# A deformable convolution's gathers on GpSimd: the limit on items under way counts landed gathers, two items back, in place of PE's turns, and the buffers' wait is written out in every item

## The chip, the cores and the metric

One core of a Trainium2 chip. Times are microseconds of device time for one execution. The kernel before takes 948.3 us, the median of three runs (947.69 to 948.37).

## What is computed

Input x is float32, 4 images of 128 channels by 48 x 48. Cut to what matters:

```python
def deform(x):                       # x normalised by groups of 4 channels
    om = conv3x3(x, w_offset) + b_offset          # 27 channels: dy, dx, mask of 9 taps
    py, px = grid_y + dy, grid_x + dx             # a place for each pixel and tap
    cols = bilinear(x, py, px) * sigmoid(mask)    # four corners, weighted
    out = einsum('bckhw,ock->bohw', cols, w_conv) + b_conv
    return relu(batchnorm(out))                   # statistics over all images

x = x + deform(groupnorm(x))
x = x + conv3x3(groupnorm(x), w) + b
```

## The kernel before, in words

The pixels of the four images are cut into 24 chunks of 384 (three tiles of 128 pixels). The host lays out a table with one row for each place of the padded image; a row holds the 128 channels of all four corners of that place, 2 KB. For one tap and one tile of 128 pixels a single indirect DMA, issued by GpSimd (L388), gathers 128 such rows into the buffer `g[:, k, t]`, 256 KB. There are 9 x 3 such buffers, so one chunk fills all of them, and the whole kernel makes 648 gathers.

An **item** is three gathers whose sums are made together. In chunks 1 to 22 an item is one tap of all three tiles, nine items to a chunk. In chunk 0 and in chunk 23 (`BY_TILE`) an item is three taps of one tile, and the last chunk has ten items, as its last three taps are split 2 and 1. All items are counted through from 0 to 216; `first_item(c)` is the number of a chunk's first.

For each item, in this order:

- GpSimd issues the three gathers; their landing adds to the semaphore `gathered[i]`, one for each place i in the chunk. `landed(c, i)` is the value that it has when item i of chunk c is there.
- The vector engine (`sum_item`) multiplies three corners by their weights in place (L952), ScalarE the fourth (`scale_item`, L682), both after waiting for `gathered[i]`. Then the vector engine adds the four (L965, L968, L971) into `acc`, one of five. Each item adds 4 to `sum_step`.
- PE turns the sums by transposing (`turn_item`, L507) and adds 1 to `turned`; ScalarE copies them into `cols` (L663); PE multiplies them by the weights (`conv_item`, L495) one or two items later.

Beside the items, between their steps, the vector engine works out the places and weights of the next chunk (L847 to L883 for chunks 0 and 1, `later_indices` after that), and PE the offsets' convolution (L443). Those orders are written out by hand and are the same before and after.

GpSimd's queue is strictly in order. At a chunk's first item it waits for the chunk's indices (`idx_ready` for chunks 0 and 1, after that a value of `sum_step` in item 3 of the chunk before). At an item it waits, if need be, for `sum_step`, so that the sums that read the buffers it takes are done: in chunk 1 these are the sums of items 6 to 8, for the first item those of item 6; between later chunks it is the item nine back, and in chunk 23 it is three to seven back. Lastly it waits for `turned`: item s starts when item s-4 is turned (`LEAD = 4`). As a turn comes after its item's sums, the wait for `sum_step` is left out where the wait for `turned` covers it, which is nearly everywhere.

SP loads x: image 0 first, then the weights, then images 1, 2 and 3 (1152 KB each, L341; each of them waits for the one before it) and the second convolution's weights (L342), while the first gathers are under way.

When all items are done, the batch statistics, the ReLU, the second group normalisation and the second convolution follow (from about 830 us), in a form with four products for two columns; GpSimd then mixes columns (L327) and adds (L319).

Of the kernel before, what the change touches and what calls it, by code (L numbers as in the profile page):

```python
# [34 lines left out]

TILE_ROWS = 3

LEAD = 4

SUMS, TURNS = 5, 3  # L40

# [44 lines left out]
def items(c):  # L86

    if c not in BY_TILE:
        return [[(k, t) for t in range(TILES)] for k in range(TAPS)]
    return [[(k, t) for k in taps] for t in range(TILES) for taps in (LAST_SETS if (c, t) == (ALL - 1, TILES - 1) else TAP_SETS)]  # L90


def first_item(c):
    return sum(len(items(i)) for i in range(c))


def all_items():
    return [(c, i) for c in range(ALL) for i in range(len(items(c)))]
# [6 lines left out]
def last_use(c, unit):  # L105

    return next(i for i, units in enumerate(items(c)) if unit in units)
# [6 lines left out]
def sums_at(c, i, slot=3):  # L114

    return 4 * item(c, i) + slot + 1
# [22 lines left out]
def landed(c, i):  # L139

    return 16 * sum(len(items(e)[i]) for e in range(c + 1) if i < len(items(e)))
# [21 lines left out]
def build(nc, x_d, tab_d, woff_d, wconv_d, w1_d, boff_d, par_d, grid_d, out_d):  # L163

    with ExitStack() as ctx:
# [6 lines left out]
        def sem(name):  # L172
            return ctx.enter_context(nc.semaphore(name))
# [95 lines left out]
        gathered = [sem(f"gathered{i}") for i in range(max(len(items(c)) for c in range(ALL)))]  # L269
        scaled = sem("scaled")  # L270
        sum_step = sem("sum_step")
        turned = sem("turned")
# [44 lines left out]
        def add_band(eng, b, j):  # L317
            s = b * HW + j * BP
            return eng.tensor_tensor(x[:, s:s + BP], x[:, s:s + BP], o[:, s:s + BP], ALU.add)  # L319

        def mix(eng, b, h, m):
            first, rows = (0, BR + 2) if h == 0 else (h * BR + 2, BR)
            src = xn[:, b % IMAGES * PW + first:b % IMAGES * PW + first + rows, :]
            d0, d2 = src[:, :, 0:W:2], src[:, :, 2:PW:2]
            d1, d3 = src[:, :, 1:W:2], src[:, :, 3:PW:2]
            p, q, op = ((d0, d2, ALU.subtract), (d1, d2, ALU.add), (d2, d1, ALU.subtract), (d1, d3, ALU.subtract))[m]
            return eng.tensor_tensor(mixed[:, m, first:first + rows, :], p, q, op)  # L327

        @block.sync
        def _(sp):  # L330
            for i in range(0, CHUNKS, 2):
                sp.dma_start(x[:, X0[i] * CP:X0[i + 1] * CP], x_d[:, 0, X0[i] * CP:X0[i + 1] * CP]).then_inc(x0_in[i], 16)
            sp.dma_start(woff[:], woff_d).then_inc(wo_in, 16)
            sp.dma_start(boff[:], boff_d).then_inc(wo_in, 16)
            sp.dma_start(grid[:], grid_d).then_inc(gr_in, 16)
            sp.dma_start(wconv[:], wconv_d).then_inc(wc_in, 16)
            sp.dma_start(params[:], par_d).then_inc(wc_in, 16)
            for b in range(1, B):
                if b > 1:
                    sp.wait_ge(xr_in[b - 2], 16)  # L340
                sp.dma_start(x[:, b * HW:(b + 1) * HW], x_d[:, b]).then_inc(xr_in[b - 1], 16)  # L341
            sp.dma_start(w1[:], w1_d).then_inc(w1_in, 16)  # L342
            for n in range(B * BANDS):
                sp.wait_ge(finished, 2 * n + 2)
                sp.dma_start(out_d[:, n * BP:(n + 1) * BP], x[:, n * BP:(n + 1) * BP]).then_inc(stored, 16)
            sp.wait_ge(stored, 16 * B * BANDS)

        @block.gpsimd
        def _(pl):
            xn4 = xn[:].rearrange("p (b r) w -> p b r w", b=IMAGES)  # L350
            pl.memset(wz[:], 0.0).then_inc(consts, 1)
            pl.memset(eps[:], EPS).then_inc(consts, 1)
            pl.memset(last_stats[:, 0:1], float(B * HW - 2 * P)).then_inc(consts, 1)
            pl.memset(gshift[:], 0.0).then_inc(consts, 1)
            pl.memset(gavg[:], 1.0 / GROUP).then_inc(consts, 1)
            pl.memset(ident[:], 0.0).then_inc(consts, 1)
            gv = gavg[:].rearrange("p (a b) -> p a b", b=GROUP)
            pl.wait_ge(consts, 5)
            pl.affine_select(out=gv, in_=gv, compare_op=ALU.is_ge, fill=0.0, base=0,
                             pattern=[[-GROUP, P // GROUP], [0, GROUP]], channel_multiplier=1).then_inc(consts, 1)  # L360
            pl.wait_ge(consts, 7)
            pl.affine_select(out=gv, in_=gv, compare_op=ALU.is_ge, fill=0.0, base=GROUP - 1,  # L362
                             pattern=[[GROUP, P // GROUP], [0, GROUP]], channel_multiplier=-1).then_inc(consts, 1)
            pl.affine_select(out=ident[:], in_=ident[:], compare_op=ALU.not_equal, fill=1.0, base=0,
                             pattern=[[-1, P]], channel_multiplier=1).then_inc(consts, 1)
            pl.memset(xn4[:, :, 0:PW:PW - 1, :], 0.0).then_inc(consts, 1)
            pl.memset(xn4[:, :, 1:1 + H, 0:PW:PW - 1], 0.0).then_inc(consts, 1)

            for c in range(ALL):
                if c < 2:  # L370
                    pl.wait_ge(idx_ready, 2 * c + 1)
                else:
                    pl.wait_ge(sum_step, sums_at(c - 1, *IDX_SLOT))
                for i, units in enumerate(items(c)):
                    if c == 0 and i == len(TAP_SETS):
                        pl.wait_ge(idx_ready, 2)
                    if c:

                        used = max(last_use(c - 1, unit) for unit in units)
                        if i < len(items(c - 1)):  # L380
                            used = max(used, i)
                        if first_item(c - 1) + used > first_item(c) + i - LEAD:
                            pl.wait_ge(sum_step, (first_item(c - 1) + used + 1) * 4)
                    if first_item(c) + i >= LEAD:

                        pl.wait_ge(turned, first_item(c) + i - LEAD + 1)
                    for k, t in units:
                        pl.indirect_dma_start(  # L388
                            out=g[:, k, t].rearrange("p q c -> p (q c)"), out_offset=None, in_=tab_d,
                            in_offset=bass.IndirectOffsetOnAxis(ap=idx[:, c % 2, t, k:k + 1], axis=0),  # L390
                        ).then_inc(gathered[i], 16)

            def add(b):
                for j in range(0, BANDS, 2):
                    pl.wait_ge(relued, b * BANDS + (BAND_ORDER.index(j) + 1))
                    add_band(pl, b, j).then_inc(added, 1)

            def mix_band(b, h):
                pl.wait_ge(normed, b * BANDS + (h + 1))
                if b:  # L400

                    pl.wait_ge(conv1, MIX * ((b - 1) * BANDS + min(h + 2, BANDS)))
                for m in range(MIX):
                    mix(pl, b, h, m).then_inc(mixed_ready, 1)

            add(0)
            for b in range(B - 1):
                mix_band(b, 1)
                mix_band(b, 2)
                add(b + 1)  # L410
                mix_band(b, 3)
                mix_band(b + 1, 0)
            for h in range(1, BANDS):
                mix_band(B - 1, h)
# [711 lines left out]
```

## Time and profile before

| what | before |
|---|---|
| median of 3 runs | 948.3 us |
| the profiled execution | 948.03 us |
| its span, first to last instruction | 946.3 us |
| busy, PE / vector engine / ScalarE / GpSimd | 748.1 / 795.8 / 375.0 / 669.2 us |
| GpSimd's gathers (L388), 648 | 613.3 us busy, 212.9 us idle ahead of them |
| moved by the gathers' queue | 169.91 MB |
| first and last gather start | 16.09 and 828.58 us |

The span is cut by what the trace records; the execution's own time is 1.7 us longer. A row of the profile for a group of instructions gives the line, engine and operation, what is written and read, the count, busy time, the mean of one in ns, and the idle time of that engine just before, with what ended most of it. A timeline row gives start, duration, engine, line, operation, operands, count, and in brackets the idle time before and its releaser; "issue" is idle time in which the engine waited for nothing that the profile shows. "DMA to landing" is the time from a gather's start on GpSimd until its data is there and its semaphore raised.

### The profile page before, as it was taken

To read this page: it belongs to the slowest core of one execution; us is meant where nothing else is said; L and a number is where in the kernel's file an instruction comes from. 1 tells how busy PE (TensorE), PEld (TensorE's weight loads), DVE (VectorE), ACT (ScalarE), POOL (GpSimd) and SP (SyncE) were. 2 spreads that over 40 slices of the span, in tenths; PEclk is the share of its full clock that TensorE was granted. 3 is DMA by queue.
4 is the path that set the end of the run, shared out by engine and by line. 5 is a ranking of instruction groups with operands and counts; after the bars stand their busy time and mean duration, and the time that the engine had idled before them with its cause. 6 is when DMAs were issued, how large, how long until landed. Compare 5 with 4: busy or idle time off the path is not lost.

```text
span 946.3 us, 8953 instructions
## 1 busy us (share of the span) xinstructions
PE 748.1 (79%) x2436; PEld 351.1 (37%) x2436; DVE 795.8 (84%) x1533; ACT 375.0 (40%) x1026; POOL 669.2 (71%) x731
## 2 busy tenths in 40 slices
PE   7688778877877877787778788778678776879998
PEld 5342322322322322232223323223222222667776
DVE  3789989888889989888899899888889889866664
ACT  3433435434333435433434345343343344453210
POOL 3777777777777777777777777777777777737551
PEclk9876778878768778976887878787797785599999
DMA  7777777777777777777777777777777777711111
GB/s 274 233 200 209 211 210 210 210 209 212 209 211 211 209 212 209 212 209 210 210 210 210 210 212 210 210 212 209 211 209 211 209 210 211 210 33 51 51 51 50
DMA packets 56246, 181.39 MB, mean 192 GB/s; under 512 B 11012, under 2 KB 12036, under 8 KB 55812
## 3 DMA queue, kind: packets, MB, share of 16 engines
q0 software_dynamic: 51840, 169.91, 62.5%
q1 hardware_dynamic: 3924, 10.32, 2.9%
q10 hardware_dynamic: 432, 0.59, 0.2%
q8 instruction: 19, 0.31, 0.1%
q14 instruction: 31, 0.25, 0.1%
HBM read 176.06 MB, written 4.72 MB: 191 GB/s over the span
## 4 chain that ended last, share of the span: by engine, by line
POOL 36%; PE 18%; DVE 18%; issue 14%; DMA 12%; ACT 1%; DVEq 0%; POOLq 0%; ACTq 0%
POOL g L388 36%; DMA g<-corner_table,idx 12%; DVE g L952 7%; PE TP L593 2%; PE PA L593 2%; PE CO L593 2%; PE CO L495 2%; PE TP L507 2%; DVE PA L965 2%; DVE PA L968 2%; DVE acc L971 2%; PE OMT L443 2%; PE VU L593 1%; PE OMT L593 1%; PE PA L438 1%
## 5 line engine op out<-in xcount | busy, mean ns | idle before, releaser
L388 POOL DMA_INDIRECT g<-corner_table,idx x648 | 613.3, 947 | 212.9 <-issue 180.7
L682 ACT ACTIVATE PA<-g,wt 128x128 f32<-128x128 f32 x642 | 203.4, 358 | 459.1 <-DMA g<-corner_table,idx 256.1
L952 DVE TENSOR_TENSOR g<-g,PA 128x1152 f32<-128x1152 f32 (+1 forms) x217 | 291.4, 1343 | 51.5 <-DMA g<-corner_table,idx 50.9
L495 PE MATMUL CO<-cols,wcs 128*128 128x384 f32 (+1 forms) x504 | 260.2, 619 | 78.7 <-ACT cols L663 77.5
L507 PE MATMUL TP<-ident,acc 128*128 128x128 f32 x648 | 146.9, 347 | 101.3 <-DVE acc L971 98.7
L443 PE MATMUL OMT<-xn,woff 128*27 128x384 f32 (+2 forms) x450 | 187.3, 534 | 3.2 <-DVE wt L878 2.0
L495 PEld LDWEIGHTS CO<-cols,wcs 128*128 128x128 f32 x504 | 92.8, 238 | 223.5 <-ACT cols L663 193.7
L507 PEld LDWEIGHTS TP<-ident,acc 128*128 128x128 f32 x648 | 89.1, 171 | 224.9 <-DVE acc L971 211.3
L965 DVE TENSOR_TENSOR PA<-g,PA 128x384 f32<-128x384 f32 x214 | 120.6, 564 | 19.1 <-ACT PA L682 1.2
L968 DVE TENSOR_TENSOR PA<-g,PA 128x384 f32<-128x384 f32 x214 | 119.8, 560 | 5.9
L971 DVE TENSOR_TENSOR acc<-g,PA 128x384 f32<-128x384 f32 x214 | 118.0, 552 | 5.9
L663 ACT ACTIVATE cols<-TP 128x384 f32<-128x384 f32 (+1 forms) x217 | 101.3, 467 | 8.8 <-PE TP L507 8.6
L443 PEld LDWEIGHTS OMT<-xn,woff 128*27 128x27 f32 x450 | 38.9, 110 | 67.5 <-issue 62.4
L327 POOL TENSOR_TENSOR g<-xn 128x288 f32<-128x288 f32 (+1 forms) x60 | 41.4, 724 | 31.7 <-ACT xn L769 30.6
L481 PE MATMUL CO<-vt,ut 9*128 9x384 f32 (+1 forms) x56 | 38.5, 784 | 0.0
L646 ACT ACTIVATE std<-OMT,eps 128x1 f32<-128x1 f32 x4 | 1.0, 262 | 50.4 <-PE OMT L424 50.4
L438 PE MATMUL PA<-gavg 128*128 128x128 f32 x128 | 18.1, 305 | 2.9 <-POOL gavg L362 2.6
L319 POOL TENSOR_TENSOR x<-x,o 128x576 f32<-128x576 f32 x8 | 12.1, 1524 | 10.8 <-ACT o L757 10.7
L438 PEld LDWEIGHTS PA<-gavg 128*128 128x128 f32 x128 | 17.2, 217 | 3.1 <-POOL gavg L362 2.6
L464 PE MATMUL VU<-ident,vsum 128*9 128x128 f32 x72 | 12.2, 279 | 6.5 <-DVE g L952 5.7
L481 PEld LDWEIGHTS CO<-vt,ut 9*128 9x128 f32 x56 | 12.9, 284 | 9.4 <-issue 9.4
L451 PEld LDWEIGHTS OMT<-ident,om 27*128 27x128 f32 x72 | 8.3, 179 | 20.2 <-issue 19.2
(148 smaller groups left out, 525.9 us busy)
## 6 DMA issues: line engine op xcount, KB each, us to landing
g<-corner_table,idx POOLq DMA_INDIRECT x648, 3.7
out_dram<-x SPq DMA_DIRECT2D x16, 288.0 KB, 2.1
x<-x_dram SPq DMA_DIRECT2D x3, 1152.0 KB, 7.8
x<-x_dram ACTq DMA_DIRECT2D x3, 192.0 KB, 4.2
x<-x_dram SPq DMA_DIRECT2D x3, 192.0 KB, 3.9
wconv<-wconv_dram SPq DMA_DIRECT2D x1, 576.0 KB, 5.0
w<-w_dram SPq DMA_DIRECT2D x1, 576.0 KB, 10.0
grid<-grid_dram SPq DMA_DIRECT2D x1, 162.0 KB, 4.2
```

What stands on the lines that cost most here:

```text
L388: pl.indirect_dma_start(out=g[:, k, t].rearrange("p q c -> p (q c)"), out_offset=None, in_=tab_d, in_offset=bass.IndirectOffsetOnAxis(ap=i ...
L443: last = nc.tensor.matmul(OM[:, first * W:(first + rows) * W], woff[:, k, :], xn[:, row + k // 3:row + k // 3 + rows, k % 3:k % 3 + W], st ...
L481: nc.tensor.matmul(co_bank(c, t)[:, lo:hi], ut[:, c // CHUNKS % 2, :], vt[:, lo:hi], start=True, stop=False)
L495: last = nc.tensor.matmul(co_bank(c, t)[:, t * P:t * P + size], wcs[:, c // CHUNKS % 2, k, :], cols[:, s % TURNS, n * P:n * P + size], sta ...
L507: last = nc.tensor.transpose(TP[s % 2][:, n * P:(n + 1) * P], acc[:, s % SUMS, n, :], ident[:])
L593: last = nc.tensor.matmul(MX[h % 2][m][:, 0:HB], w, mixed[:, m, r:r + BR, :], start=(ky == 0), stop=(ky == 2))
L663: nc.scalar.activation(cols[:, s % TURNS, 0:size], TP[s % 2][:, 0:size], ACT.Copy).then_inc(copied, 1)
L682: last = nc.scalar.activation(first[:, n] if s < LAST_SUMS else g[:, k, t, 0, :], g[:, k, t, 0, :], ACT.Copy, scale=wt0[:, c % 2, t, k:k + 1])
L952: nc.vector.tensor_tensor(corners[:, :, 1:4, :], corners[:, :, 1:4, :], weights[:, :, 1:4].unsqueeze(3).to_broadcast([P, size, 3, P]), ALU ...
L965: nc.vector.tensor_tensor(some, corners[:, :, 1, :], some, ALU.add).then_inc(sum_step, 1)
L968: nc.vector.tensor_tensor(some, corners[:, :, 2, :], some, ALU.add).then_inc(sum_step, 1)
L971: nc.vector.tensor_tensor(acc[:, s % SUMS, 0:size, :], corners[:, :, 3, :], some, ALU.add).then_inc(sum_step, 1)
```

## The change

The wait for `turned` goes. In its place an item waits until the item two back has landed (`AHEAD = 2`), whichever chunk that is in. The wait for `sum_step` stands in every item from chunk 1 on, without the test that left it out. Gathers, their order, their number and all other engines' programs stay as they are.

```diff
-LEAD = 4
+AHEAD = 2
...
+            order = all_items()
             for c in range(ALL):
                 if c < 2:
                     pl.wait_ge(idx_ready, 2 * c + 1)
...
                     if c:
 
                         used = max(last_use(c - 1, unit) for unit in units)
                         if i < len(items(c - 1)):
                             used = max(used, i)
-                        if first_item(c - 1) + used > first_item(c) + i - LEAD:
-                            pl.wait_ge(sum_step, (first_item(c - 1) + used + 1) * 4)
-                    if first_item(c) + i >= LEAD:
-
-                        pl.wait_ge(turned, first_item(c) + i - LEAD + 1)
+                        pl.wait_ge(sum_step, (first_item(c - 1) + used + 1) * 4)
+                    s = first_item(c) + i
+                    if s >= AHEAD:
+
+                        pl.wait_ge(gathered[order[s - AHEAD][1]], landed(*order[s - AHEAD]))
                     for k, t in units:
                         pl.indirect_dma_start(
...
```

## Rows read from the trace of the kernel before

**Rows 1.** Page, the costliest groups

```profile
L388 POOL DMA_INDIRECT g<-corner_table,idx x648 | 613.3, 947 | 212.9 <-issue 180.7
```

**Rows 2.** Busy time by stage: PE, PEld, DVE, ACT, POOL, clock, DMA share, GB/s

```profile
100.00:200.00 100.00, 76.80 (x235) 29.97 (x235) 89.09 (x172) 44.56 (x124) 75.63 (x81) 0.81 0.74 210
```

**Rows 3.** Timeline of GpSimd, line 388

```profile
18.75 0.95 POOL L388 DMA_INDIRECT g<-corner_table,idx  x1 [0.30 <-issue]
...
23.75 0.95 POOL L388 DMA_INDIRECT g<-corner_table,idx  x1 [0.30 <-issue]
...
36.74 0.95 POOL L388 DMA_INDIRECT g<-corner_table,idx  x1 [2.04 <-PE TP L507]
...
52.98 0.94 POOL L388 DMA_INDIRECT g<-corner_table,idx  x1 [1.54 <-issue]
...
119.25 0.95 POOL L388 DMA_INDIRECT g<-corner_table,idx  x1 [0.30 <-issue]
...
120.50 0.94 POOL L388 DMA_INDIRECT g<-corner_table,idx  x1 [0.30 <-DVE g L952]
...
828.58 0.95 POOL L388 DMA_INDIRECT g<-corner_table,idx  x1 [0.30 <-issue]
```

**Rows 4.** Timeline of the other engines, 26 to 52 us

```profile
26.61 1.36 DVE L952 TENSOR_TENSOR g<-g,PA 128x1152 f32<-128x1152 f32 x1 [3.81 <-DMA g<-corner_table,idx]
...
35.98 0.49 PE L507 MATMUL TP<-ident,acc 128*128 128x128 f32 x3
...
39.53 1.35 DVE L952 TENSOR_TENSOR g<-g,PA 128x1152 f32<-128x1152 f32 x1
...
41.56 0.56 DVE L965 TENSOR_TENSOR PA<-g,PA 128x384 f32<-128x384 f32 x1 [0.68 <-ACT PA L682]
...
51.66 0.55 DVE L971 TENSOR_TENSOR acc<-g,PA 128x384 f32<-128x384 f32 x1
```

**Rows 5.** Line 388 by source: landing of all; of the gather at 18.75; at 22.50

```profile
DMA to landing us min/median/max: 3.3/3.7/7.8
...
DMA to landing us min/median/max: 7.8/7.8/7.8
...
DMA to landing us min/median/max: 6.7/6.7/6.7
```

**Rows 6.** Timeline around a late landing

```profile
614.50 0.96 POOL L388 DMA_INDIRECT g<-corner_table,idx  x1 [0.30 <-issue]
...
619.52 0.95 POOL L388 DMA_INDIRECT g<-corner_table,idx  x1 [0.30 <-PE TP L507]
...
620.26 1.35 DVE L952 TENSOR_TENSOR g<-g,PA 128x1152 f32<-128x1152 f32 x1 [1.95 <-DMA g<-corner_table,idx]
```

**Rows 7.** Line 388 by source: nine stretches of 34 us, from 84 us on

```profile
DMA to landing us min/median/max: 3.5/3.7/4.8
...
DMA to landing us min/median/max: 3.4/3.7/4.7
...
DMA to landing us min/median/max: 3.4/3.7/5.4
...
DMA to landing us min/median/max: 3.4/3.7/4.4
...
DMA to landing us min/median/max: 3.5/3.7/4.6
...
DMA to landing us min/median/max: 3.5/3.7/4.4
...
DMA to landing us min/median/max: 3.5/3.7/5.0
...
DMA to landing us min/median/max: 3.5/3.6/5.7
...
DMA to landing us min/median/max: 3.4/3.7/4.9
```

**Rows 8.** DMA queues, 614 to 622 us: packets, MB, share

```profile
q8 instruction: 1, 0.02, 0.7%
```

## The prediction

> **What bounds the kernel now.** I read the page first: GpSimd's line 388, 648 indirect gathers at 947 ns with 0.30 us of idle ahead of each, is the costliest group, and only its "issue" idle is large [rows 1]. Then the table by stage: from 100 to 200 us GpSimd runs 81 gathers at 75.6%, while the vector engine is busy 89%, PE 77% and the DMA engines 74% [rows 2]. Eighty-one gathers in 100 us is one per 1.25 us (0.95 busy and 0.30 of issue), and the timeline shows that pitch, as from 119.25 to 120.50 [rows 3]. So the stage of the gathers, 16 to 830 us, is bound by GpSimd making descriptors. Everything else is paced by it. From the gather at 52.98 to the last at 828.58 there are 620 pitches, 775.0 us at 1.25; the trace has 775.6. The stage thus holds 0.6 us of stalls after 53 us, and two larger ones ahead of that: 2.04 - 0.30 = 1.74 us at 36.74 (item 5, put down to PE's turn) and 1.54 - 0.30 = 1.24 us at 52.98 (item 9, the first of chunk 1) [rows 3]. That is all an easier limit could win. Anything that stalls GpSimd afterwards is lost for good, as it has no slack.
>
> **What the change removes.** Item s no longer waits for the turn of item s-4. In chunk 0 that frees 1.74 us at item 5. But item 9 takes buffers that item 6 has to be done with, a wait that stands before and after. Item 6's last addition starts at 51.66 and takes 0.55, so it ends at 52.21, and the gather starts at 52.98 [rows 3, 4]. The vector engine goes from 39.53 to there nearly without a pause (four items' sums and chunk 1's indices). So item 9 could not have started sooner than 52.98, however early items 5 to 8 were: the 1.74 us are worth nothing. Of the 0.6 us left I take 0.2 as winnable.
>
> **What it adds at the start.** Item 2 now waits until item 0 has landed. Item 0's third gather starts at 18.75 and lands 7.8 us later, at 26.55, while the ordinary gather takes 3.7 [rows 3, 5]; the vector engine's wait for it ends at 26.61 [rows 4]. The large loads of x lie beside it, in both kernels. Item 2 started at 23.75 before [rows 3]. A released gather starts some 0.27 us after its releaser: item 5 did, after a turn that began at 35.98 and took 0.49 [rows 3, 4]. Item 2 then starts at 26.55 + 0.28 = 26.83, a new stall of 3.08 us. Item 1's last gather, issued at 22.50, lands at 29.2 [rows 5], ahead of item 3's place at 30.58: no second stall. From 26.83, item 9's first gather (21 pitches of 1.25 on) is due at 53.08, not 52.98. The vector engine moves too: item 4's third gather starts at 36.83 and lands at 40.53, so its first product starts at 40.55 in place of 39.53 [rows 4]. Before, its second step was held to 41.56 by ScalarE; now it comes at 40.55 + 1.35 + 0.11 = 42.01, so the later chain moves by 0.45 and item 6's sums end at 52.66. If the gather follows that by the same 0.77 us as before (52.98 - 52.21), item 9 starts at 53.43. **Term: +0.45 us** (bounds +0.1, at the pitch alone, to +0.5).
>
> **What the written-out buffer wait costs.** From chunk 1 on nearly every item then has two waits in place of one. Where both are satisfied early I cost this at nothing: the first item of a chunk has two waits already, and its gather at 120.50 comes 1.25 us behind the one at 119.25, like any other [rows 3]. What covers it is GpSimd working on the gather before. If the cover were gone, 200 items would pay each time. What the buffer wait asks for, sums nine items back, is long done except at item 9.
>
> **What the new limit costs in steady state.** Item s-2's third gather starts four pitches, 5.00 us, ahead of item s. If released late, item s starts a lag after the landing. The nearest rows for the lag are two: 0.27 us at item 5, which has one wait, and 0.77 us at item 9, which has several and was released by one that is not the gather's own [rows 3, 4]. I take 0.77, as from chunk 1 on each item has two waits and the new one is written second, as the wait that released item 9 was. The Trainium skill's page "Perfetto Trace Analysis", section "Identifying Dependency Chains", says that instructions with several waits may get separate EventSemaphore instructions ahead of them; by that the second wait is one more step for the queue after its release, and the 0.77 agrees.
>
> With 0.77 a gather may take 4.23 us to land before it stalls the item two behind. The ordinary 3.7 is hidden. But nine stretches of 34 us after chunk 0 have a maximum above that: 4.8, 4.7, 5.4, 4.4, 4.6, 4.4, 5.0, 5.7 and 4.9 us [rows 7]. Read one by one, each is the third gather of its item, the one with the least room. The worst starts at 614.50; the vector engine waits for it until 620.26, while item 160 had started at 619.52, so the new wait would have held that one [rows 6]. These are no accidents of one run, I think: in this stretch one 16 KB packet of the instruction queue q8 passes the DMA engines [rows 8], and the same goes for eight of the nine; I take it for an engine's program being loaded, and only GpSimd's program changes, so they should return at about the same items. Sum: 43.9 - 9 x 4.23 = **+5.8 us**. With the lag of 0.28 the limit is 4.72 and five remain, 0.08 + 0.68 + 0.28 + 0.98 + 0.18 = +2.2 us. With a lag of 1.0, near ordinary landings of 4.0 to 4.2 count too: replaying all 648 starts and landings gives +8.5.
>
> The sum: 0.45 + 5.8 - 0.2 = +6.0 us. The profiled execution took 948.03 us (span 946.3), 0.27 below the median of 948.3. The stage after 830 us starts on the last item and only moves along. 948.03 + 6.0 = **954.0 us**, 0.6% more.
>
> **Rivals.** (a) *Short lag.* The queue sees the landing as fast as item 5 saw its turn: 0.45 falls to 0.1, 5.8 to 2.2, so 948.03 + 2.1 = 950.1. For it speaks item 5, against it item 9. It decides at items 42, 86, 115 and 131, which would show no stall. (b) *Ordinary landings are caught too.* If the lag is 1.0 or more, or the delays fall on more items, the sum is +8.5 and the time 956.5. For it: the room is only 5.00 - 3.7 - 0.77 = 0.5 us; against it, nothing in the trace shows a lag over 0.77. (c) *No change.* Landings are in time everywhere, and GpSimd keeps its 1.25: the start costs 0.1, 0.2 is won, 948.0 to 948.5. The mechanism's place is the room of 5.00 us: it decides if no third gather takes over 4.2. Against it stand the nine maxima, unless these were chance. The Trainium skill's "DMA: Bandwidth & Descriptors", section "Anatomy of one DMA", gives a transfer on this path as 2.0 us plus bytes over 436e3; by that, an estimate from its figures, a gather of 262144 bytes lands in 2.6 us and the wait is never late. The rows have 3.7 with outliers to 5.7, which decide against it. (d) *Faster.* There would have to be more than 0.6 us to win after 53 us, or a vector engine that reaches item 6's sums sooner; at most 947.4. No row speaks for it.
>
> **How the numbers follow.** Chances: the forecast (lag 0.5 to 0.9) 0.55; (a) 0.19; (b) 0.12; (c) 0.11; (d) 0.03. A difference of 0.2%, 1.9 us, is about what a measurement of this kernel tells from none, so the line to slower is 950.2. The forecast and (b) are wholly slower, and half of (a) is: 0.55 + 0.12 + 0.10 = 0.77; within 0.2%: the other half of (a), (c) and most of (d), 0.21; faster 0.02. The range goes from (a) at its low side, 949.9, to (b) with 1 us of noise in how many late landings one run has, 957.5; (c) and (d) are left out.
>
> **What would show it.** In the changed profile: item 2's first gather at about 26.8 with some 3.1 us of idle, and none at item 5; item 9 at 53.1 to 53.4; GpSimd's waits naming its own gathers instead of PE's turns; eight to ten stalls of 0.2 to 1.5 us at the first gather of items two behind a late landing (25, 42, 70, 86, 115, 131, 140, 160, 176); the last gather at 834 to 835 in place of 828.58. The pitch elsewhere stays 1.25 and the stretch from the last gather to the end keeps its length. A pitch above 1.25 at every third gather would prove me wrong on the cost of a second wait, and stalls at many items with 3.7 us landings would prove me wrong on the lag.

## The result, and the profile after

The changed kernel takes 955.94 us, the median of five runs (952.68 to 956.26), where before takes 948.37 (947.69 to 949.8): a ratio of 1.0074, with a 95% interval of 1.0057 to 1.0091. It is slower, by 0.7%, some 7 us. The profiled execution is the quickest of the five, 952.68 us with a span of 950.7; that is 4.65 us above the profiled one of before, and 3.3 below its own median.

The page has the same busy times as before. What changed is how GpSimd's idle time ahead of its gathers ends [rows 1], and the chain that ended last: GpSimd had 36% of it and the gathers' transfers 12%; now they have 14% and 46%. The first fence is from the page of the changed kernel, the chain by engine and the group of the gathers; the second is the list of its waits on GpSimd (us in total, times, longest us).

```profile
DMA 46%; DVE 18%; POOL 14%; PE 12%; issue 9%; ACT 1%; POOLq 0%; DVEq 0%; ACTq 0%
...
L389 POOL DMA_INDIRECT g<-corner_table,idx x648 | 613.4, 947 | 217.8 <-issue 136.9
```

```profile
POOL g L389 <- issue: 136.9, 446, 0.6
POOL g L389 <- DMA g<-corner_table,idx: 49.3, 146, 3.0
```

Idle time rose by only 4.9 us, from 212.9 to 217.8. Of the 49.3 us put down to transfers, most is 0.30 us at a time, the ordinary pitch with the landing named as releaser. So the shares of the chain mislead here; what counts is where a pitch is longer than 1.25 us. The timeline of the changed kernel on GpSimd shows it, with the first products of two items and the sum that item 9 waited for (these answer to [rows 3, 4, 6]):

```profile
26.60 1.35 DVE L953 TENSOR_TENSOR g<-g,PA 128x1152 f32<-128x1152 f32 x1 [3.43 <-DMA g<-corner_table,idx]
26.77 0.94 POOL L389 DMA_INDIRECT g<-corner_table,idx  x1 [2.95 <-DMA g<-corner_table,idx]
...
53.44 0.55 DVE L972 TENSOR_TENSOR acc<-g,PA 128x384 f32<-128x384 f32 x1
...
54.75 0.94 POOL L389 DMA_INDIRECT g<-corner_table,idx  x1 [2.03 <-DVE acc L972]
...
617.62 0.96 POOL L389 DMA_INDIRECT g<-corner_table,idx  x1 [0.30 <-DMA g<-corner_table,idx]
...
623.13 1.35 DVE L953 TENSOR_TENSOR g<-g,PA 128x1152 f32<-128x1152 f32 x1 [1.70 <-DMA g<-corner_table,idx]
623.87 0.94 POOL L389 DMA_INDIRECT g<-corner_table,idx  x1 [1.55 <-DMA g<-corner_table,idx]
...
833.64 0.95 POOL L389 DMA_INDIRECT g<-corner_table,idx  x1 [0.88 <-DMA g<-corner_table,idx]
```

Item 2 starts at 26.77, just after item 0's landing. Item 9 starts at 54.75 in place of 52.98. The gather at 617.62 is the third of item 158, the one that was late before too; it lands at 623.11, when the vector engine starts on it, and item 160 starts 0.76 us later, at 623.87, with 1.25 us of stall. The last gather starts at 833.64, 5.06 us later than the 828.58 of before. By the starts of all 648 gathers:

| stretch | later than before, us |
|---|---|
| first gather (16.47, was 16.09) | 0.38 |
| from there to item 9's first | 1.39 |
| first gathers of later items, sum of their pitches less 1.25 each (3.33, was 0.45) | 2.88 |
| second and third gathers, the same (0.56, was 0.15) | 0.41 |
| sum | 5.06 |

Five of the later items hold 2.1 us: 86, 115, 146, 160 and 176, each two behind a late third gather. Item 216, the last, holds 0.58 us more; why is told further below.

### The profile page after: what moved, and what is told of

It reads as the page before. It is cut to its first block, busy times and chain, and to the rows that moved or that the text cites. A ratio compares the mean times of both kernels' runs of the same rounds, so it can differ in the third digit from the quotient of the medians.

```text
span 950.7 us, 9138 instructions
## 1 busy us (share of the span) xinstructions
PE 748.7 (79%) x2436; PEld 351.3 (37%) x2436; DVE 796.4 (84%) x1533; ACT 375.1 (39%) x1026; POOL 669.3 (70%) x731
## 4 chain that ended last, share of the span: by engine, by line
DMA 46%; DVE 18%; POOL 14%; PE 12%; issue 9%; ACT 1%; POOLq 0%; DVEq 0%; ACTq 0%
DMA g<-corner_table,idx 46%; POOL g L389 14%; DVE g L953 7%; PE TP L594 2%; PE PA L594 2%; PE CO L594 2%; DVE PA L966 2%; DVE PA L969 2%; DVE acc L972 2%; PE VU L594 1%; PE OMT L594 1%; DVE bst L835 1%; PE PA L439 1%; PE CO L496 0%; ACT PA L683 0%
## 5 line engine op out<-in xcount | busy, mean ns | idle before, releaser
L389 POOL DMA_INDIRECT g<-corner_table,idx x648 | 613.4, 947 | 217.8 <-issue 136.9
```

The source lines that it names most:

```text
L389: pl.indirect_dma_start(out=g[:, k, t].rearrange("p q c -> p (q c)"), out_offset=None, in_=tab_d, in_offset=bass.IndirectOffsetOnAxis(ap=i ...
```

## The experiments

Ratios are to the kernel before on the same chip. Kernels 1 to 4 shared a chip and its runs of before, as did 5 to 8, and 9 to 12.

**1 and 2. The order of the two waits, and the written-out wait alone.** In the compiled program an item's first wait sits in the gather instruction itself, and the others in a separate semaphore instruction ahead of it. In the changed kernel from chunk 1 on the gather holds the buffers' wait and the separate instruction the landing.

```diff
                 for i, units in enumerate(items(c)):
+                    s = first_item(c) + i
+                    if s >= AHEAD:
+                        pl.wait_ge(gathered[order[s - AHEAD][1]], landed(*order[s - AHEAD]))
...
                         pl.wait_ge(sum_step, (first_item(c - 1) + used + 1) * 4)
-                    s = first_item(c) + i
-                    if s >= AHEAD:
-                        pl.wait_ge(gathered[order[s - AHEAD][1]], landed(*order[s - AHEAD]))
```

The chunk's wait for indices moves behind the landed one as well, so that this is first at every item.

> The changed kernel with its two kinds of waits in the other order: in each item the wait for the landing is written first and so becomes the gather's own wait, and the buffers' wait becomes the separate instruction ahead of it. Theory (a late landing costs its lateness plus the lag of the queue, and the lag is 0.75 us behind a separate wait but 0.27 behind the gather's own): lag 0.25 to 0.3 at late items, only landings over 4.7 us cost, and the time is 2 to 4 us below the changed kernel, 951 to 953.5. Rival A (a landed wait costs the same wherever it stands): within 1 us of the changed kernel, 955 to 957, lag still 0.75. Rival B (the start in chunk 0 makes the loss): the same as the changed kernel, since chunk 0 has one wait in both.

Measured: 950.73 us, ratio 1.0027 (1.0015 to 1.004); the loss falls from 7 to under 3 us. The program has the same instructions, and only the order of two waits differs. Its timeline around the same late gather, the third of item 158:

```profile
616.04 0.95 POOL L389 DMA_INDIRECT g<-corner_table,idx  x1 [0.31 <-issue]
...
621.54 1.35 DVE L953 TENSOR_TENSOR g<-g,PA 128x1152 f32<-128x1152 f32 x1 [1.86 <-DMA g<-corner_table,idx]
621.78 0.94 POOL L389 DMA_INDIRECT g<-corner_table,idx  x1 [1.03 <-DMA g<-corner_table,idx]
```

The landing is as late (5.5 us), but item 160 follows it by 0.26 us and not by 0.76. Its four stalls behind a late landing (items 25, 70, 115 and 160) all have that lag, and the changed kernel's all have 0.76. (The trace has landings to 0.01 us; the view gives them to 0.1.) Rivals A and B fall.

The second kernel goes back to PE's turns, with `pl.wait_ge(turned, s - LEAD + 1)` at `LEAD = 4` for the landed wait and the rest of the change kept.

> One part alone: the limit by PE's turns, four items back, as before, with the buffers' wait written out in every item. So nearly every item has a separate wait for turns and an own wait for sums. Theory: written-out waits cost nothing when they are satisfied early, but at each chunk's item 6 the turn comes only just in time before, and behind a separate wait a lag of 0.75 in place of 0.27 makes stalls there: up to 22 times 0 to 0.5 us, 949 to 956, pitch elsewhere 1.25. Rival C (the added instructions themselves cost queue time): every third pitch is longer than 1.25 by the same amount, some 0.01 us or more at all 190 items. If neither, 948.4.

Measured: 948.16 us, ratio 1.0001 (0.9989 to 1.0013), no difference from before, and the pitch is 1.25 at the items as elsewhere. So the written-out wait costs nothing, and rival C falls. But the first part of the expectation was a miss. I had read pitches 0.02 us too long at seven of the chunks' items 6 as turns that come just in time; had they been that, the longer lag would have stalled each by some 0.5 us. One item in the trace was stalled, item 74 (297.75 us), by 1.05 us: the turn of item 70 came late and ended at 296.97, so here a turn behind a separate wait has the long lag too, 0.78 us.

**3 and 4. No limit at all, and the limit one item wider.** The third leaves out the two lines of the landed wait, the fourth has `AHEAD = 3`.

> The changed kernel without the landed wait: only the buffers' wait, written in every item. Theory (before had at most 0.6 us of stalls after item 9, and item 9 is held by item 6's sums): 947.7 to 948.5, no measurable difference from before; item 5 without a stall, item 9's first gather still at 52.5 to 53.5. Rival D (the limit on items under way was protecting something, such as the landings from crowding): landings longer than 3.7 us in the median and a time over 949.

> The changed kernel with the landed wait three items back in place of two, nothing else. The third gather of item s-3 starts 8.75 us ahead of item s; at a lag of 0.75 it may take 8.0 us. Theory: no landing is that late, item 3 may just pass (item 0 has landed by 26.6, its place is 27.5 to 27.9); 948 to 948.8. Rival A or C (a cost at each wait, late or not): it stays above 953.

Measured: 947.86 us, ratio 1.0003 (0.9993 to 1.0013), and 947.86, ratio 1.0007 (0.9993 to 1.002). Both are as before. Late third gathers are there all the same: six of 4.9 to 5.7 us without any limit. No gather waits on them, so they cost nothing. Item 9 started at 51.31 us, sooner than the 52.5 to 53.5 expected. The median landing is 3.7 us with and without a limit, so it protects nothing. One item more of room takes the whole loss away, though every item has the same two waits. In the fourth's list of waits on GpSimd, the landing is named 145 times, never for more than the pitch's 0.3 us:

```profile
POOL g L389 <- issue: 138.6, 449, 2.1
POOL g L389 <- DMA g<-corner_table,idx: 44.2, 145, 0.3
```

**5, 6 and 7. The changed kernel again, and its two halves.** `if s >= AHEAD and not c` keeps the landed wait in chunk 0 alone, `if c` keeps it everywhere else.

> The changed kernel once more, beside the next three on the same chip, for runs and a second trace of it. Theory: 953 to 957; stalls again at the items two behind the late third gathers (of items 23, 40, 68, 84, 113, 129 or 144, 158, 174), with a lag of 0.75, and again 3 us at item 2. Rival (late landings are chance): stalls at other items.

> The landed wait in chunk 0 alone; from chunk 1 on only the buffers' wait. Theory: what item 2's stall of 3 us costs after the slack ahead of item 9 has taken up its part: by the traces without and with it, item 9 starts 34.8 and 36.4 us after the first gather, so 1 to 1.8 us over the kernel without any limit (947.9): 948.5 to 949.7, not measurably or barely slower than before. Rival B (the start makes the loss): 952 or more.

> The mirror of that: no landed wait in chunk 0, the changed kernel's in all later chunks. Theory: late landings behind a separate wait make most of the loss, 4 to 6 us: 952 to 954.5. Rival B: 948 to 949.

| kernel | median, us | ratio | 95% interval |
|---|---|---|---|
| changed, again | 956.2 | 1.0069 | 1.0053 to 1.0084 |
| landed wait in chunk 0 alone | 949.8 | 1.0007 | 0.9997 to 1.0018 |
| landed wait after chunk 0 alone | 954.49 | 1.0047 | 1.0029 to 1.0065 |

The later chunks make the loss, 4.5 of 6.2 us; rival B falls. The start is worth between nothing and 2 us: its kernel can't be told from before, and the difference of the other two, 1.7 us, is within their intervals. In the trace of the sixth, item 2 starts at 25.56 with a stall of 1.5 us, half of the 3 us expected, as item 0 had landed at 25.30, and item 9 starts 35.70 us after the first gather, where before had 36.89. The second trace of the changed kernel has stalls at items 42, 70, 78, 86, 115, 131, 146, 160, 176 and 191, all with a lag of 0.76 us, and 4.2 us of them in all, with 0.67 more at item 216. All but 78 and 191 are where the theory or the first trace has one; item 25, which the theory named, has none.

**8. One item back.** `AHEAD = 1`.

> The changed kernel with the landed wait one item back, so that it stops every item and the lag can be read 200 times. Theory: from chunk 1 on an item takes 2.5 us to its third gather, 3.3 to 3.7 to the landing and 0.75 of lag, 6.55 to 6.95 in place of 3.75; in chunk 0, with one wait, 0.27. Time 948 + 208 x (2.8 to 3.2) + 8 x 2.5: 1550 to 1635. Rival A (the same lag everywhere): chunk 0 and later ones show one lag; at 0.27 everywhere the time is 1450 to 1540.

Measured: 1647 us. From chunk 1 on the lag from landing to the next item's start is 0.76 us (median of 208 places). In chunk 0 it is 0.26 at seven of eight items, and 0.77 at item 3, which has a second wait, the one for the indices. An item takes 6.96 us in the median, 2.50 + 3.7 + 0.76, and 7.01 in the mean, as some land later or are followed by up to 1.1 us; the mean's 3.26 us over 3.75 brings the time above the 1635 that 3.2 gave. Two items' starts from GpSimd's timeline, the first after a late landing, the second an ordinary one (the idle time stands in brackets, and the pitch within an item stays 1.25):

```profile
811.23 0.94 POOL L389 DMA_INDIRECT g<-corner_table,idx  x1 [5.09 <-DMA g<-corner_table,idx]
812.48 0.95 POOL L389 DMA_INDIRECT g<-corner_table,idx  x1 [0.30 <-issue]
813.73 0.95 POOL L389 DMA_INDIRECT g<-corner_table,idx  x1 [0.31 <-issue]
817.95 0.95 POOL L389 DMA_INDIRECT g<-corner_table,idx  x1 [3.26 <-DMA g<-corner_table,idx]
```

**9 and 10. Where the late gathers come from.** Ahead of the first turn PE makes 5 or 10 more products, `if (c, k) == (0, 0): warm_up(5, TP[1])`; nobody reads them.

> The changed kernel with 5 more 128x128 products (10 more PE instructions with their weight loads) ahead of the first turn, in PE's idle time; nothing reads their result. In all traces so far the late third gathers are those of items 23, 40, 68, 84, 97, 113, 129, 144, 158, 174 or 189, mostly 14 to 17 apart. Theory (a block of PE's program is loaded there, and PE runs some 22 instructions to an item): they come half an item, 1 to 2 gathers, earlier. If they are then first or second gathers, with 1.25 to 2.5 us more room, the loss falls from 6 to 2 to 4 us over before, 950 to 953. Rival E (the place is set by GpSimd's own program or by its descriptor ring): the same items, the same third gathers, 955 to 957.

> The same with 10 more products (20 instructions). Theory: late gathers some 2 to 3 gathers ahead of their old places, about one item earlier, so again third gathers of the items before (22, 39, 67, 83, 112, 143, 157, 173) or first ones of the same item; 953 to 957. Rival E: the same items as before. The products also keep PE busy ahead of the first turn, so the half-speed stretch from 29 us may end sooner and item 9 start up to 1 us earlier.

Measured: 955.0 us, ratio 1.0065 (1.005 to 1.0079), and 954.63, ratio 1.0055 (1.0041 to 1.0069). The items whose third gather took 4.4 us or more:

| kernel | items |
|---|---|
| before | 23 40 68 84 113 129 138 158 174 |
| changed | 84 113 144 158 |
| turns, written out | 23 40 68 84 113 144 158 189 |
| no limit | 40 84 97 113 144 158 |
| one item wider | 23 40 68 84 129 144 158 189 |
| changed, again | 68 84 113 144 158 174 189 |
| one item back | 30 39 112 188 |
| 5 more products | 23 37 68 82 143 172 205 |
| 10 more products | 36 50 111 156 187 203 |
| 10 more products, no limit | 21 36 50 111 144 153 187 |

Nothing in GpSimd's program was touched, and most of the places moved by one to four items (with 5 more, 23 and 68 stayed; with 10 more the move is two to four items, more than the one expected). They moved with the packets of queue q8: one passed at 110 to 112 us in the second trace of the changed kernel, and with 10 more products at 100 to 102. One late landing of that kernel, from its timeline, its landings between 154 and 168 us (this gather is the maximum), and its queues from 158 to 162 us (packets, MB, share):

```profile
156.73 0.95 POOL L389 DMA_INDIRECT g<-corner_table,idx  x1 [0.30 <-DMA g<-corner_table,idx]
...
162.59 0.95 POOL L389 DMA_INDIRECT g<-corner_table,idx  x1 [1.15 <-DMA g<-corner_table,idx]
```

```profile
DMA to landing us min/median/max: 3.3/3.7/5.1
```

```profile
q8 instruction: 1, 0.02, 2.7%
```

The gather at 156.73, the third of item 36, lands at 161.83, and item 38 starts 0.76 us later. Rival E falls: the place is set by PE's program. The kept traces show it a second way. For four packets of q8, the table has the time, the number of PE's products started by then, and the item of the last gather that GpSimd had started:

| kernel | times, us | products | items |
|---|---|---|---|
| before | 110.4, 173.9, 219.6, 279.5 | 335, 479, 589, 710 | 24, 41, 53, 69 |
| one item back | 175.4, 294.4, 384.7, 491.2 | 335, 478, 591, 709 | 22, 39, 52, 67 |
| 10 more products | 101.9, 158.5, 212.7, 272.4 | 342, 462, 588, 717 | 22, 37, 51, 67 |

With one item back, GpSimd takes nearly twice as long for an item and PE's program is as before: the packets keep to PE's count. In every trace 19 pass, and after the start one passes for about 125 products. That it carries a block of PE's program is the plainest reading. The half that would have helped did not come: the loss stayed.

Why always the third gather? A good part of it is how a landing is counted. The three gathers of an item raise one semaphore, by 16 each, and the first one's landing is read at the 16th increment, the second's at the 32nd. One missing increment of either is soon made up in the count by those of the next gather. Only behind the third do none follow. In the trace of before, item 158's third gather starts at 614.50; of the item's 48 increments 47 are there by 618.08, and the last comes alone at 620.24. Over all traces, where a packet starts 2.0 to 2.75 us after a gather does, third gathers land after 4.9 us (median of 35), first ones after 4.2 (22) and second ones after 4.1 (31), none of these above 4.5. So a late first or second gather can't be told from its reading. It costs an item nothing until it is later than the item's last increment. That these gathers are delayed as much as third ones is not shown.

**11 and 12. Both costs reduced, and no limit with PE kept busy.** The eleventh is the first with `if c` for the landed wait, the twelfth the third with the 10 products.

> The changed kernel with both of its costs reduced: no landed wait in chunk 0, and the landing as the gather's own wait later. Theory (the two costs add, 1.6 us of the start and some 3 of the separate wait): only landings over 4.7 us are left, 0.5 to 3 us over the kernel before, 949 to 951.5 at a before of 948 to 950. If one of the two was mis-read, it stays 4 us or more over before.

> Without any limit (as the third experiment), with the 10 more products ahead of the first turn. If PE's half-speed stretch at 29 to 35 us delays item 6's sums and with them item 9, holding its clock up gains 0 to 1.5 us: 946.5 to 948.5 where before gives 948. Nothing else in the stage of the gathers can be won, since the pitch of 1.25 us is GpSimd's.

Measured: 951.05 us, ratio 1.002 (1.0006 to 1.0033), and 947.97, ratio 0.9995 (0.9984 to 1.0006). The eleventh is no better than the first's 1.0027 beyond the intervals; its five stalls behind landings of 4.9 to 5.7 us, all with a lag of 0.26, make some 2.6 us, and its item 9 came late, at 37.11 us from the first gather, without any landed wait ahead of it. The twelfth is not measurably faster than before: PE does stay at its upper level until 41 us, and item 9 comes at 34.63 us from the first gather, the soonest of all, but the two microseconds are within what runs differ by. No kernel of this study is measurably faster than the kernel before; its bound is the pitch of GpSimd's 648 gathers.

## Why the prediction was right, and where its terms were off

**What bounds the kernel.** Right. The pitch stayed at 1.25 us in every trace, and without any limit the time was 947.86 us.

**The lag.** The step on which the sum hung. Read from one row each, 0.27 and 0.77 us, it measured 0.26 and 0.76 in 216 places, and 0.76 at the five stalls after the change. The first experiment turned it from the one into the other by the order of two lines, and the time fell to 950.73; rival (a) had 950.1 for that lag. The rule of the Trainium skill's "Perfetto Trace Analysis", section "Identifying Dependency Chains", that further waits may become separate EventSemaphore instructions, holds in the compiled program; that being held in one costs 0.5 us more is what the runs add.

**The late gathers, +5.8 us.** Right in kind, with places forecast one by one. Mis-sized for the profiled execution: the stalls there make 2.1 us, at four of the nine forecast items (86, 115, 160, 176) and at item 146, where eight to ten stalls were forecast, and 4.2 us in the second trace. The term went by the landings of one trace, and how much is late differs much between traces. The same sum, what third gathers after chunk 0 took above 4.24 us, is 5.8 us for that trace; over all fourteen it is 2.2 to 6.0, with a median of 4.1. How late a given gather is differs from run to run (item 68's took 5.4 us before, under 4.3 in the first trace after, 5.5 in the second). The half after chunk 0 alone measured +4.5 us in the median. The remark that each late gather is the third, "the one with the least room", was right, but it says less than it seems to, by the way landings are counted.

**The start, +0.45 us.** Too small for the profiled execution, where it was 1.39, and its way was only partly seen. Item 2 stood still as forecast (26.77 where 26.83 was said), though its stall was 2.65 us and not 3.08, as the first gather, and with it item 2's place, came 0.38 us later. But I moved the vector engine's chain alone. In the trace after, PE ran at the lower of its two levels (granted clock 0.50, that is 1.2 GHz) from 28.9 to 39.2 us in one piece. Before it did so from 28.1 to 35.0 and again from 45.2 to 48.6: as long in all, 10.2 us, but not at the same items. The row is from the changed kernel's busy time by stage, with the clock third from its end:

```profile
35.00:39.00 4.00, 4.00 (x14) 2.51 (x14) 2.48 (x4) 1.29 (x4) 3.06 (x4) 0.50 0.76 218
```

Before, the same stretch had 1.00 and 22 of PE's instructions in place of 14. The copies that PE's turns release held ScalarE, and ScalarE held the vector engine's second steps, as here at item 4, where 42.01 was forecast:

```profile
41.70 0.49 ACT L664 ACTIVATE cols<-TP 128x384 f32<-128x384 f32 x1 [2.66 <-PE TP L508]
...
43.52 0.56 DVE L966 TENSOR_TENSOR PA<-g,PA 128x384 f32<-128x384 f32 x1 [1.43 <-ACT PA L683]
```

Item 6's sums ended at 53.99 us, in place of 52.21. That the clock set this chain back is read from one pair of traces, not shown by a run. The tenth kernel, with the landed wait and 10 more products, runs PE at the upper level until 41.7 us, and its item 9 comes 36.56 us after the first gather; the changed kernel's two traces have 38.28 and 35.88. Over thirteen traces (all but the eighth experiment's) PE's time at half speed between 26 and 52 us is 3.4 to 13.7 us, and item 9 starts 34.6 to 38.3 us after the first gather, with and without the landed wait (36.98 and 37.11 in two kernels without it in chunk 0, 35.70 to 38.28 with it). Seven of them have 10.2 us at half speed, and item 9 still lies anywhere from 35.70 to 38.28. So the start's own part stays open, between 0 and 2 us.

**Item 5's 1.74 us are worth nothing.** Right in the time: no limit, 1.0003. The reason was too strict, though. Item 9 can start sooner than 36.89 us after the first gather, as 34.80 without any limit shows, where PE was at half speed for 3.4 us only; the runs' spread swallows it.

**Written-out waits at nothing.** Right, by the second experiment: 1.0001.

**A place I had not seen.** The last chunk's items have 3, 2 and 1 gathers. Item 216 waits for item 214, whose third gather starts only three pitches ahead, at 829.32, and lands at 832.88, 3.56 us later. The last gather starts 0.76 us after that, 0.58 behind its place; in the second trace it is 0.67. It costs nothing: item 216's product starts at 838.20, behind item 215's, when its data has been there since 836.88. So the end moved by 4.37 us (the first ReLU from 838.50 to 842.87) where the last gather moved by 5.06.

**The sum.** 954.0 was forecast and 955.94 measured, in the range. The mechanism is the one forecast, but that the sum comes so close is in part luck: in the profiled execution the start cost three times its term (1.39 for 0.45) and the late gathers less than half of theirs (2.1 for 5.8). That execution moved by less than the sum of 6.0, 4.65 us, and the median by more, 7.6 us. Both traces of the changed kernel are of the quickest run of their set, so what the slower runs had more, some 3 us, no trace shows.

## What to carry to other kernels

Where the bound is a queue that has no slack, a limit on what is under way must have more room than the slowest landing, not than the median one: here 5.00 us of room less 0.76 of lag passed the 3.7 us of nearly all gathers, and the few above 4.2 made most of the loss (4.5 of 6.2 us), while one item more of room took the whole of it to nothing. Read the largest landings and how they lie to the item, not only the mean, and read them from more than one trace. And where a gather of GpSimd has several waits, write first the one that is likely to come last, so that it becomes the instruction's own: it starts 0.26 us after its release and not 0.76.

## What the runs showed of the hardware that I had not expected

- A wait in a separate instruction ahead of a gather costs GpSimd 0.50 us more from release to start (0.76 to 0.26), and nothing measurable when it is satisfied early: 184 more of them left the time at a ratio of 1.0001.
- The gathers that land late (4.4 to 5.8 us for 3.7) come at much the same items from run to run and from kernel to kernel, 84 of 88 third ones beside a 16 KB packet of an instruction queue. They move when ten or twenty instructions are added to PE's program, and follow PE's count of products when GpSimd is slowed down. The kernel before has them as well and doesn't notice.
- Three gathers that raise one semaphore hide a late increment of the first two: in item 158, 47 of 48 increments were there 2.16 us ahead of the last. Of the landings read at 4.4 us or more after chunk 0 all but four, at 4.4 to 4.5, are third ones, in part for that reason.
